# The feed-forward tail: residual rows added by TensorE, outputs moved to ScalarE and GpSimd, all rows normalised on ScalarE

## What is computed

```python
x = x + _L0_xattn_ref(_layernorm(x), ctx_1024, mask, ...)   # cross-attention, 16 heads
x = x + _L0_attn_ref(_layernorm(x), ...)   # state-space block: y = scan(...) * silu(z); x + y @ out_proj
x = x + _L0_ffn_ref(_layernorm(x), w_gate, w_up, w_down)

# in _L0_ffn_ref
gate = jax.nn.silu(_bitlinear(x, w_gate))      # 256 -> 1024
up = _bitlinear(x, w_up)                       # 256 -> 1024
return _bitlinear(gate * up, w_down)           # 1024 -> 256
```

## Time and profile before

| | |
|---|---|
| median of 3 runs | 412.8 us (412.78 to 412.99) |
| the profiled execution | 412.8 us, span 411.0 us |
| busy, share of the span | PE 356.3 us (87%), DVE 346.9 (84%), POOL 285.5 (69%), ACT 278.5 (68%) |
| costliest groups | L1885 POOL 149.4 us, L1591 DVE 142.7, L750 PE 72.0, L1172 ACT 74.8 |
| the chain that ended last, by engine | PE 33%, DVE 24%, issue 15%, ACT 13%, POOL 12% |
| DMA | 22.4 MB, mean 55 GB/s |

### The profile page before, as it was taken

How to read it: one execution, slowest core, us unless ns; L and a number is a source line. 1 busy time by engine, 2 the same in 40 slices (tenths; PEclk the granted TensorE clock), 3 DMA queues, 4 the chain that set the end, 5 groups by cost and what they waited for, 6 DMA issues and landing times.

```text
span 411.0 us, 8655 instructions
## 1 busy us (share of the span) xinstructions
PE 356.3 (87%) x2864; PEld 241.3 (59%) x2868; DVE 346.9 (84%) x723; ACT 278.5 (68%) x596; POOL 285.5 (69%) x333
## 2 busy tenths in 40 slices
PE   3889999998998999985898999898899778789684
PEld 1557767574766674553465566566666556457352
DVE  1468888778889787968999999989999999988795
ACT  1266679758975895289879879767874553265564
POOL 0046475646557563237999999999999699976820
PEclk9999999999999999999999999999999999999989
DMA  5981010101010000008600000375000000000001
GB/s 192 383 350 53 1 53 3 53 13 41 12 43 2 2 3 0 0 6 230 181 2 0 2 5 26 88 190 134 2 0 2 1 2 0 2 0 2 13 27 65
DMA packets 22623, 22.41 MB, mean 55 GB/s; under 512 B 1042, under 2 KB 20242, under 8 KB 22068
## 3 DMA queue, kind: packets, MB, share of 16 engines
q1 hardware_dynamic: 22020, 21.39, 16.5%
q10 hardware_dynamic: 560, 0.48, 0.3%
HBM read 20.75 MB, written 1.12 MB: 53 GB/s over the span
## 4 chain that ended last, share of the span: by engine, by line
PE 33%; DVE 24%; issue 15%; ACT 13%; POOL 12%; DMA 1%; DVEq 0%; POOLq 0%; PEldq 0%; ACTq 0%
DVE both L1591 9%; POOL both L1885 8%; PE ps L536 8%; PE ps L505 4%; PE ps L750 3%; PE ps L488 3%; PE ps L740 3%; ACT both L1172 2%; DVE both L1415 2%; PE ps L523 2%; PE ps L566 2%; ACT both L1007 2%; PE ps L553 2%; ACT both L1158 1%; PE ps L599 1%
## 5 line engine op out<-in xcount | busy, mean ns | idle before, releaser
L1885 POOL TENSOR_TENSOR both<-both 128x1024 f32<-128x1024 f32 x64 | 149.4, 2367 | 0.2
L1591 DVE TENSOR_TENSOR_SCAN both<-both,ps 128x1024 f32<-128x1024 f32 x64 | 142.7, 2271 | 4.6 <-PE ps L740 4.6
L1831 POOL TENSOR_SCALAR both<-both,rden 128x256 f32<-128x256 f32 x128 | 62.0, 500 | 62.9 <-DVE rden L1422 62.9
L1172 ACT ACTIVATE both<-delta,a_neg 128x504 f32<-128x504 f32 x120 | 74.8, 704 | 11.0 <-DVE both L1591 11.0
L750 PE MATMUL ps<-con,both 128*128 128x128 f32 x512 | 72.0, 279 | 7.8 <-POOL both L1885 7.6
L1007 ACT ACTIVATE both<-both,negmax 128x256 f32<-128x256 f32 x128 | 63.3, 498 | 17.9 <-DVE negmax L1415 17.9
L750 PEld LDWEIGHTS ps<-con,both 128*128 128x128 f32 x512 | 56.1, 141 | 30.0 <-issue 16.0
L740 PE MATMUL ps<-both 32*128 32x256 f32 x512 | 45.7, 426 | 10.3 <-DVE both L1591 7.8
L1415 DVE CUSTOM_DVE_ANT_0 both<-ps,both 128x256 f32<-128x256 f32 x128 | 46.9, 417 | 6.7 <-PE ps L488 5.5
L536 PE MATMUL ps<-both 128*128 128x512 f32 x64 | 34.0, 656 | 8.2 <-DMA both<-in_ctx_t 6.8
L505 PE MATMUL ps<-con,both 128*128 128x128 f32 x256 | 38.2, 275 | 0.0
(11 more groups left out here) (149 smaller groups left out, 607.6 us busy)
## 6 DMA issues: line engine op xcount, KB each, us to landing
both<-bounce SPq DMA_DIRECT2D x16, 512.0 KB, 6.3
both<-in_ctx_t SPq DMA_DIRECT2D x8, 512.0 KB, 3.5
both<-in_wg SPq DMA_DIRECT2D x1, 1024.0 KB, 8.3
both<-in_wu SPq DMA_DIRECT2D x1, 1024.0 KB, 10.8
both<-in_wd SPq DMA_DIRECT2D x1, 1024.0 KB, 12.8
win_sb<-in_win SPq DMA_DIRECT2D x1, 1024.0 KB, 14.7
resid<-in_x SPq DMA_DIRECT2D x1, 896.0 KB, 6.5
both<-in_wkv SPq DMA_DIRECT2D x1, 512.0 KB, 4.4
```

Of the source, the lines that this page charges most:

```text
L1172: act.activation(da[sl % 2].rearrange("p (a s n t) -> p a s n t", a=GT, n=HN, s=2)[:, :, :, n, 1:L], delta[:, idx % RING_D].rearrange("p ( ...
L1591: dve.tensor_tensor_scan(h_sb[:, hu % RING_H], da[e.slot % 2][:, e.tt * HU:(e.tt + 1) * HU], bank(inflow_bank(hu), 2), 0.0, ALU.mult, ALU. ...
L1831: pool.tensor_scalar(s, s, rden[:, u, q:q + 1], 1.0, ALU.mult, ALU.mult).then_inc(normed, 1)
L1885: pool.tensor_tensor(g_sb[:, hu % RING_G].rearrange("p (n s t) -> p s n t", n=HN, s=2), h_sb[:, hu % RING_H].rearrange("p (s n t) -> p s n ...
```

## The change

- `add_scan` is gone from VectorE. `out_proj_of` adds a fifth product, identity by `resid`, so that PSUM holds the sum, and `copy_x2` on ScalarE copies two tiles at once from PSUM to `resid` (now it releases `x2_ready`). For group 0 the copies stand between the halves of slot 12 and after `round_input(1)`.
- All rows are normalised on ScalarE; GpSimd makes only the offset (`offset_input`) for tiles 3 to 7.
- `product` takes the up scale in, so `inner_scale` has two small instructions in place of three, and `round_inner` waits for the second.
- Outputs 0 to 5: ScalarE scales the product out of PSUM (`scale_down`), GpSimd adds `resid` (`add_rows`). Outputs 6 and 7 stay on VectorE. TensorE may reuse the PSUM region after `scale_down`.
- A Silu of one column (`f_warm`) stands ahead of the tail on ScalarE.
- The orders of the calls on TensorE, ScalarE, VectorE and GpSimd are changed to suit.

The core of the diff:

```diff
             def out_proj_of(g, tt, k):
+                pe.wait_ge(resid_ready, count(NT))
                 pe.wait_ge(x2_ready, count(g * GT + tt // 2 * 2))
                 pe.wait_ge(yz_sb, count(g * GT + tt + 1))
                 for c in range(NC):
                     mm = pe.matmul(bank(k)[:, tt % 2 * D:(tt % 2 + 1) * D], yz[:, tt % 2, c * P:(c + 1) * P],
-                                   wout_sb[:, c], start=c == 0, stop=c == NC - 1)
+                                   wout_sb[:, c], start=c == 0, stop=False)
+                mm = pe.matmul(bank(k)[:, tt % 2 * D:(tt % 2 + 1) * D], ident, resid[:, g * GT + tt], start=False, stop=True)
...
             def down(t):
-                pe.wait_ge(f_out, count(t if t < 3 else t - 1))
+                held = t if t < 3 else t - 1
+                pe.wait_ge(f_scaled, count(min(held, NT_POOL)))
+                if held > NT_POOL:
+                    pe.wait_ge(f_out, count(held - NT_POOL))
...
 (TensorE's order)
             up(2)
             out_proj_of(1, 0, 3)
+            turn_gated(1, 2, 2, (yz_sb, GT + 2))
             out_proj_of(1, 1, 3)
             turn_input(3, 4)
-            turn_gated(1, 2, 2, (yz_sb, GT + 2))
             activations(0)
...
             out_proj_of(1, 3, 3)
+            down(0)
             turn_input(4, 4)
-            down(0)
             gates(4)
             up(4)
             activations(2)
+            down(1)
             turn_input(5, 4)
-            down(1)
+            gates(5)
             activations(3)
-            gates(5)
...
+            def copy_x2(g, half):
+                act.wait_ge(outproj_ready, count(g * GT + 2 * half + 2))
+                t = g * GT + 2 * half
+                act.activation(resid[:, t:t + 2].rearrange("p t d -> p (t d)"), bank(SPARE_BANK if g == 0 else 3),
+                               ACT.Copy).then_inc(x2_ready, 2)
...
-            slot(12)
+            half_slot(12, 0)
+            copy_x2(0, 0)
             stage_xc(7, (x2_ready, 2))
+            half_slot(12, 1)
             slot(13)
...
+            def scale_down(t):
+                act.wait_ge(f_down, count(t + 1))
+                act.wait_ge(f_os, count(t + 1))
+                act.wait_ge(stored[t % 2], count(t // 2 * 16))
+                act.activation(f_o[t % 2][:], f_down_ps(t), ACT.Copy, scale=f_s2[t][:, C_OUT:C_OUT + 1]).then_inc(f_scaled, 1)
+
+            act.activation(f_warm[:], eps[:], ACT.Silu).then_inc(passed, 1)
...
 (ScalarE's order)
             copy_yz(1, 0, 2)
+            normal_input(3)
             silu_gate(2)
             copy_yz(1, 1, 2)
             round_inner(1)
+            copy_yz(1, 2, 2)
+            copy_x2(1, 0)
             round_inner(2)
             copy_input(3, 4)
-            copy_yz(1, 2, 2)
             copy_inner(0)
+            copy_yz(1, 3, 2)
             silu_gate(3)
-            copy_yz(1, 3, 2)
+            normal_input(4)
+            copy_x2(1, 1)
             copy_inner(1)
+            normal_input(5)
             round_inner(3)
             copy_input(4, 4)
             silu_gate(4)
+            scale_down(0)
             copy_inner(2)
+            normal_input(6)
             copy_input(5, 4)
+            scale_down(1)
             copy_inner(3)
             silu_gate(5)
             round_inner(4)
+            normal_input(7)
             copy_input(6, 4)
+            scale_down(2)
             silu_gate(6)
             round_inner(5)
             copy_input(7, 4)
             copy_inner(4)
+            scale_down(3)
             silu_gate(7)
             round_inner(6)
             copy_inner(5)
+            scale_down(4)
+            round_inner(7)
             copy_inner(6)
-            round_inner(7)
+            scale_down(5)
             copy_inner(7)
...
-                dve.tensor_tensor(f_gu[t % 2], bank(0, 2), f_sg[t % 2], ALU.mult).then_inc(f_gu_ready, 1)
+                dve.wait_ge(*weights_scaled(t))
+                dve.scalar_tensor_tensor(f_gu[t % 2], bank(0, 2), f_s[t][:, C_SU:C_SU + 1], f_sg[t % 2], ALU.mult, ALU.mult
+                                         ).then_inc(f_gu_ready, 1)
...
 (VectorE's order)
             inner_to_bf16(1)
-            add_scan(1, 0)
             ffn_statistics(4)
             ffn_statistics(5)
             inner_to_bf16(2)
...
             inner_scale(3)
+            ffn_statistics(6)
             input_scale(5)
-            add_scan(1, 1)
-            ffn_statistics(6)
             inner_to_bf16(3)
-            output(0)
             ffn_statistics(7)
-            input_scale(6)
             product(4)
             largest(4)
             inner_scale(4)
-            output(1)
-            input_scale(7)
+            input_scale(6)
             product(5)
-            output(2)
             largest(5)
             inner_scale(5)
             inner_to_bf16(4)
+            input_scale(7)
             product(6)
...
+            def add_rows(t):
+                pool.wait_ge(f_scaled, count(t + 1))
+                pool.tensor_tensor(f_o[t % 2][:], f_o[t % 2][:], resid[:, t], ALU.add).then_inc(f_out_pool, 1)
...
 (GpSimd's order)
             scale_weights_of(6)
+            add_rows(0)
             scale_output(4)
             round_input(7)
             scale_weights_of(7)
+            add_rows(1)
             scale_output(5)
+            add_rows(2)
             scale_output(6)
+            add_rows(3)
+            add_rows(4)
             scale_output(7)
+            add_rows(5)
```

More of the change, by code:

```diff
@@ L61 @@
 NT_ACT = 3
+NT_POOL = 6
 PE, ACTE, DVE, POOL, SP = "tensor", "scalar", "vector", "pool", "sync"
@@ L214, in build @@
         f_s2 = [sb(f"f_s2{t}", [P, 5]) for t in range(NT)]
-        f_nmean = sb("f_nmean", [P, NT_ACT])
+        f_nmean = sb("f_nmean", [P, NT])
+        f_warm = sb("f_warm", [P, 1])
         C_M2, C_CL2, C_INV2, C_A, C_OUT = range(5)
@@ L466, in _ @@
                     tile = Tile(i, c)
-                    sp.wait_ge(f_out, count(tile.t + 1))
+                    if tile.t < NT_POOL:
+                        sp.wait_ge(f_out_pool, count(tile.t + 1))
+                    else:
+                        sp.wait_ge(f_out, count(tile.t - NT_POOL + 1))
                     sp.dma_start(out[bass.ds(tile.t, 1)].rearrange("a p d -> (a p) d"), f_o[c][:]
@@ L1113, in normal_input @@
                     act.wait_ge(inproj_ready, count(NG * 2 * NC))
+                if t >= NT_ACT:
+                    if t - 2 < NT_ACT:
+                        act.wait_ge(f_hi_act, count(t - 1))
+                    else:
+                        act.wait_ge(f_hi_ready, count(t - 1 - NT_ACT))
                 act.activation(f_h[t % 2], resid[:, t], ACT.Identity, scale=s[:, C_RS:C_RS + 1],
@@ L1282, in _ @@
             round_input(1)
+            copy_x2(0, 1)
             copy_input(0, SPARE_BANK)
@@ L1295, in round_inner @@
             def round_inner(t):
-                act.wait_ge(f_a, count(t + 1))
+                act.wait_ge(f_inv2, count(t + 1))
                 act.wait_ge(f_gq, count(t - 1))
@@ L1300, in round_inner @@
                     act.activation(f_gi[t % 2][:, cols], f_gu[t % 2][:, cols], ACT.Copy,
-                                   scale=f_s2[t][:, C_A:C_A + 1], bias=MAGIC).then_inc(f_gi_ready, 1)
+                                   scale=f_s2[t][:, C_INV2:C_INV2 + 1], bias=MAGIC).then_inc(f_gi_ready, 1)
             def copy_inner(t):
@@ L1632, in copy_ut @@
                                 ).then_inc(ut_dve, 1)
-            def add_scan(g, half):
-                dve.wait_ge(resid_ready, count(NT))
-                for tt in (2 * half, 2 * half + 1):
-                    r = resid[:, g * GT + tt]
-                    dve.wait_ge(outproj_ready, count(g * GT + 2 * half + 2))
-                    dve.tensor_tensor(r, bank(SPARE_BANK if g == 0 else 3)
-                                      [:, tt % 2 * D:(tt % 2 + 1) * D], r, ALU.add).then_inc(x2_ready, 1)
             def input_row(t):
@@ L1795, in _ @@
             inner_to_bf16(5)
-            output(3)
             product(7)
-            inner_to_bf16(6)
             largest(7)
             inner_scale(7)
-            output(4)
-            output(5)
+            inner_to_bf16(6)
             inner_to_bf16(7)
@@ L1986, in _ @@
             rounded_to_bf16(2)
-            normal_input(3)
+            offset_input(3)
             round_input(3)
@@ L1991, in _ @@
             scale_output(1)
-            normal_input(4)
-            normal_input(5)
+            offset_input(4)
+            offset_input(5)
+            scale_output(2)
             round_input(4)
             scale_weights_of(4)
-            scale_output(2)
+            offset_input(6)
             round_input(5)
@@ L1999, in _ @@
             scale_output(3)
-            normal_input(6)
-            normal_input(7)
+            offset_input(7)
             round_input(6)
             scale_weights_of(6)
+            add_rows(0)
             scale_output(4)
```

41 lines of the change are left out of this document (11 added, 30 removed).

## The result

| | before | after |
|---|---|---|
| median | 412.79 us (4 runs) | 422.61 us (3 runs) |
| ratio, 95% interval | 1 | 1.0239 [1.0203, 1.0274] |
| profiled run: time, span, mean clock | 412.8, 411.0, 0.996 | 420.67, 418.9, 0.988 |
| PE, DVE, ACT, POOL busy (us) | 356.3, 346.9, 278.5, 285.5 | 361.3, 341.4, 285.3, 285.3 |

The change makes the kernel slower by 9.8 us by the medians; 421.7 was forecast, in a range of 417 to 425.

What follows compares the result with a forecast made beforehand. The later of GpSimd and VectorE paces the scan end, hand-offs among five in-order queues the tail. Placed +8.9 us, 1.87 from the scan, takes the span from 411.0 to 419.9; with 1.8 around it, 421.7 us, range 417 to 425.

Steps and rivals of the forecast that it cites:

- Scan stage: End of the scan: scan 48 starts 1.87 us later, its half slot 12 queued behind ScalarE's wait for the longer second projection.
- The rival with cover for slot 12: Scan stage: the delay of scan 48 is absorbed and only the tail is lost, 419.8 us; chance 0.12.
- the lower end of the range: Whole kernel: 416.7 us, the forecast less slot 12's cover (1.9), the clock loss (1.4) and the residual product (1.7).
- Early table load: Ahead of the tail on ScalarE: a dummy activation starts the Silu table load about 0.3 us sooner, net -0.1 us.
- The tail up to product(5): Tail replayed in queue order: gates(3) +3.9 us, product(3) +4.6, gates(4) +5.7, product(4) +3.3, product(5) at 396.24.
- silu(7), product(7): Late tail: scale_down(3), with silu_gate(7) behind it, waits for a 2.17 us store; product(7) starts 6.9 us later.
- The end: Last tail steps: output(7) starts at 415.80, +8.9 us against the old order in the same placing, 1.87 from the scan.
- the clock loss is taken to be the same in both kernels: End of the tail: the placing falls 1.4 us short of the old trace; the change adds no further clock loss.
- the third rival: Tail: the clock drops in two more spells of about 1 us each, plus the ports' 0.9: 424.6 us; chance 0.10.
- The clock's rule: TensorE in the tail: by recent busyness, gaps at 385.7, 395.1, 399.8 and 406.7 (2.3 to 3.1 us) would each cost again.
- The shared port: Tail additions on GpSimd: add_rows(1) and add_rows(5) could each take 0.46 us longer, +0.9 at most, in the upper bound.
- VectorE sets the pace: Tail rival: waits on ScalarE hide behind VectorE's work, the tail shortens by 5.4 us: 409.3 us; chance 0.10.

Runs made afterwards that it cites:

- the order whose tail had its full clock already: Kernel before with the two small scales, only row 3 normalised on ScalarE, and a new order of tail calls on all four engines: 408.15 us, ratio 0.9887.

## Why the prediction was right

Starts, measured from the end of the last weighing (placed at 366.03, in the trace 364.68), so that the scan's part is out:

| step | placed | measured | before |
|---|---|---|---|
| gates(3) start | 11.63 | 11.67 | 9.64 |
| product(3) | 16.16 | 16.13 | 13.47 |
| ScalarE idle ahead of copy_x2(1,1) | 3.5 | 3.66 | none |
| gates(4) | 22.23 | 22.29 | 18.39 |
| product(4) | 24.49 | 24.51 | 23.06 |
| product(5) | 30.21 | 30.21 | |
| add_rows(1) | 36.51 | 36.51 | |
| silu(7) | 39.83 | 39.45 | |
| product(7) | 41.00 | 40.59 | 35.99 |
| output(7) | 49.77 | 51.54 | 44.19 |

- **Scan stage**: +1.87 placed, +1.96 measured, with the idle of VectorE (2.15 us) before scan 48. The residual product is 0.43, as taken, and the parts were shown apart (1.16 and 0.80). The rival with cover for slot 12 falls. Its price was mis-sized: it and the lower end of the range take the whole 1.9 back, but with slot 12 out of the way the second longer projection delays scan 48's burst, so that only 1.16 came back. The profile names "issue" as what ended that idle, not ScalarE; only the rows of ScalarE and the run with slot 12 whole show whose it was.
- **Early table load**: -0.1 placed. The load took 1.28 us in both kernels, and the dummy 0.20; the first Silu starts 2.02 us after the start of the row's normalisation, 2.26 before. So 0.24 was saved, with nothing to see of it at the end.
- **The tail up to product(5)**: every start is within 0.1 us, ScalarE's wait before the second copy within 0.2. The new durations were right: scaling 0.47 (0.44 taken), product with the scale 1.28, copy 0.60.
- **silu(7), product(7)**: 0.4 early. The store behind which scale_down(3) waits was taken at 2.17 us; here it was issued at 401.94, and scale_down(3) started at 403.76 without a wait: 1.8 us at most. In the two runs with dummy products it took 2.8 (403.54 to 406.31) and 2.4 (403.28 to 405.65). That term varies from run to run of one kernel.
- **The end**: from product(7) to output(7) 8.77 us were placed and 10.95 measured. The 2.2 are the slow downs and transposes, where the forecast carried the 1.4 of the kernel before. With the clock full, in the two runs with dummy products, it measures 8.67 and 8.66: the placing was right and the clock wasn't in it. In the profiled run this, the store and the scan's 0.1 make +9.3 of the placed +8.9. The term that was mis-sized is "the clock loss is taken to be the same in both kernels": it was 2.3 us at the end of this tail, in one spell, against about 1 in the kernel before. In the tail that is one us more and not the two of the third rival. In the scan stage six of the seven profiled kernels with the half slot lost another 0.2 to 0.8 us behind the 2.06 us wait, and the prediction has no term for that.
- **Time and median**: the profiled run lies 1.0 us under the forecast although its difference is larger than placed. That is luck: its first 300 us took 1.44 us less than before's, and its scan stage kept the full clock. The other two runs in the median took 422.61 and 424.11 us at clocks of 0.984 and 0.976, and the median is 0.9 above the forecast. No trace of them was kept, so that a lower clock made them slower is likely and not shown.
- **The clock's rule**: it fell to 0.80 at 408 to 410 and 0.50 after that, once TensorE had been busy for only 0.67 of 2 us. That agrees with the rule of the Trainium skill (TensorE: Matmul & The Clock Gate, "What's actually happening"). But not each gap cost. The four that I named at 2.3 to 3.1 us measure 2.47, 1.82, 2.32 and 1.75 us, and the first three passed at full clock in this run; only the last, the shortest, with another 0.68 us of idle close behind it, did not. In the run with slot 12 whole TensorE did next to nothing at 396 to 398 and at 400 to 402, and the clock fell only after the second.
- **The shared port**: one of the additions, at 402.12, took 1.17 us beside a conversion on VectorE (402.00); the other five took 0.72 or 0.73, although two of them (394.87 and 401.19) ran beside a product and a reduction of VectorE. That is the extra 0.46 of the earlier trace rows, and it agrees with what the Trainium skill (SBUF — State Buffer, "SBUF: two separate sides") says of the two engines' shared pair: only some of VectorE's instructions take it, and then for the whole instruction. The prediction left this condition out. It was not on the path: the prediction's add_rows(1), which is, took 0.72.
- **VectorE sets the pace** (409.3, faster) was wrong for this order. It idled 2.6 us twice for ScalarE, and its busy time fell by 5.4 us as worked out, worth nothing. With the same parts in another order the kernel takes 409.55: so the condition of that rival, that ScalarE arrives in time, was not met here, and met to within 1.30 us there.

**What stays open.** How the 7.0 us that were placed in the tail divide among the parts: only the sums of the second half were separated (3.7 placed, 6.15 in the trace with the clock's 2.4). Outputs and normalisations lie below what the scatter lets one see, and their medians were nearer to the rival's numbers than to the placed ones. Why the clock falls after one gap and not after another isn't settled.

## What to carry to other kernels

When work is moved to an engine with idle time, write down what stands behind each new wait in that engine's queue. The idle time isn't where the work is put, and here the same work cost 10 us or gave 3, by its order (the clock's loss included). A replay of the queues with durations from the trace of before placed the changed tail to 0.1 us for its first 30 us; use it to choose the order before the change is built, not only to price it. A gap that a worse order opens on TensorE can cost a second time, through the clock; look for it in the rows behind each gap, in more than one profiled run.

## What was not expected of the hardware

- Useless products made the kernel 2 to 3 us faster (419.28 and 420.37 against 422.61), and its clock was then 0.988 to 0.995 in every run, against 0.976 to 0.988. Fewer of them gave nothing in the order whose tail had its full clock already (408.51 against 408.15).
- One wait of 2.06 us on TensorE in the scan stage was followed by half clock in six of seven profiled kernels (only after's own kept the full clock), the same wait of 0.95 us in none of seven. In the tail, waits of 1.82 to 2.47 us passed at full clock.
- At half clock a down of eight instructions takes 1.87 instead of 1.03 us and the transposes ahead of it 1.06 instead of 0.61, and these stood on the path in the last 6 us.
- The wait for a store of 128 KB, from the issue to when ScalarE may write the buffer, was at most 1.8 us in one run and 2.4 and 2.8 in two others of nearly the same kernel. The store before it, issued some 6 us earlier, took 1.83 us in all three.
